# A position-wise convolution: weights of a group in one transfer of 128 rows, four weight buffers, windows asked for in mid row

## The chip, the core and the metric

The kernel runs on one core of one Trainium2 chip. The metric is the time of one execution on the device in microseconds (us). Three runs of the kernel before took 12917.63, 12935.22 and 12935.37 us; the median is 12935.22 us.

## What is computed

The reference works on `x` of shape (32, 32, 56, 56): batch, channels, height, width. It has two residual layers. The change concerns the first, a convolution with 3 x 3 patches whose weights are not shared: each of the 56 x 56 positions has its own matrix of 32 output channels by 288 patch elements.

```python
K, STRIDE, PAD, C_IN, C_OUT, OUT_H, OUT_W, BATCH = 3, 1, 1, 32, 32, 56, 56, 32
IN_DIM, POSITIONS = C_IN * K * K, OUT_H * OUT_W
weight: (C_OUT, POSITIONS, IN_DIM)
...
patches = _unfold(x, K, STRIDE, PAD).transpose(0, 2, 1)   # batch, position, 288
out = jnp.einsum('bpi,opi->bop', patches, weight)
out = out + bias[None, :, :]
...
x = x + _L0_conv_ref(_gn(x), L0_conv_weight, L0_conv_bias)
x = x + _L1_conv_ref(_gn(x), ...)
```

`_gn` normalises each channel of each image. The second layer searches for each position the 16 nearest other positions by their channels, weighs them with a softmax, and puts the result through a matrix and a batch normalisation.

## The kernel before

The program is a chain of stages, each with its own instructions on every engine and a barrier between two of them: `normalise_input`, `convolve`, `prepare`, `split_halves`, `attend`, `normalise_output`. Only `convolve` (from L135) is changed. Everything is float32 there.

`normalise_input` leaves the normalised image in device memory as `xg`, laid out channel, row, image, column, with a border of one row and one column of zeros.

`convolve` cuts the 56 rows of the image into four quarters of 14 rows (PER = 4, QH = 14, QN = 784 positions to a quarter) and works on the same row of all four quarters at once. So the 128 partitions of a weight tile are 4 quarters (q) of 32 output channels (o). It walks 14 rows, each of 56 positions. Four neighbouring positions (SLOTS = 4), for all four quarters, are a group here; a row has 14 groups (7 CHUNKS, two groups u = 0, 1 in each), the stage 196.

What each engine does in `convolve`:

- **SP** issues all loads. At the start of a row it asks for `windows` (L198): for each of the three kernel rows k one transfer, 32 channels by 4 quarters by one padded row of 32 images (7424 bytes). Windows have two buffers, one for even and one for odd rows; the wait in L196 is for the products of the row before the one at hand. Then, for each group, it waits until the buffer of two groups ago has been turned (L202) and issues four transfers (L205), one for each quarter: 32 output channels, each with 4 x 288 numbers that lie together (4608 bytes), into 32 partitions of `w_in[:, u]`.
- **PE** waits for the group's four transfers (L240), and turns the weights, position by position, with three transposes each (L233) from 128 partitions of (q, o) to 96 partitions of (k, channel). With the turned weights as the stationary side it then multiplies (L253): for each position 12 small products, 3 kernel columns by 4 quarters, 96 rows deep, 32 output channels by 32 images. Two positions are turned ahead (AHEAD = 2), so in each group PE has 9 transposes in a row, 24 products, 3 transposes, and 72 products (the order of its instructions is the same in both kernels but for line numbers). `turned` counts turned positions; SP and ACT wait on it.
- **ACT** copies the turned weights of a position out of PSUM into `w_turned` (L272).
- **DVE** copies the results of a group from PSUM into `conv_sb` (L284), one copy for each group.
- At the end SP stores `conv_sb` in four transfers, one for each quarter (L212).

The order of the work is that of the loops as written; the engines meet at semaphores alone. SP runs as far ahead of PE as the buffers allow: `turned` starts with a credit of 2 x SLOTS (TURN_FREE, L168).

Of the kernel before, what the change touches and what calls it, by code (L numbers as in the profile page):

```python
# [5 lines left out]
FP32 = mybir.dt.float32  # L6
# [6 lines left out]
BATCH, C, H, W = 32, 32, 56, 56  # L13
N = H * W
K = 3
IN_DIM = C * K * K
NEIGHBOURS = 16
P = 128
# [116 lines left out]
def convolve(nc, weight, xg, conv):  # L135


    SLOTS = 4
    AHEAD = 2
    CHUNKS = W // (2 * SLOTS)  # L140
    KC = K * C
    with ExitStack() as stack:
        enter = stack.enter_context
        windows = enter(nc.sbuf_tensor("windows", [KC, 2, PER, BATCH * WP], FP32))
        w_in = enter(nc.sbuf_tensor("w_in", [P, 2, SLOTS, IN_DIM], FP32))
        w_turned = enter(nc.sbuf_tensor("w_turned", [KC, 4, K * P], FP32))
        conv_sb = enter(nc.sbuf_tensor("conv_sb", [P, BATCH, QN], FP32))
        ident = enter(nc.sbuf_tensor("ident_c", [P, P], FP32))
# [2 lines left out]
        ident_ready = enter(nc.semaphore("c_ident"))  # L151
        win0 = enter(nc.semaphore("c_win0"))
        win1 = enter(nc.semaphore("c_win1"))
        w0 = enter(nc.semaphore("c_w0"))
        w1 = enter(nc.semaphore("c_w1"))
        turned = enter(nc.semaphore("c_turned"))
        wt_ready = enter(nc.semaphore("c_wt_ready"))
        multiplied = enter(nc.semaphore("c_multiplied"))
# [1 line left out]
        out_stored = enter(nc.semaphore("c_out"))  # L160
        passed = enter(nc.semaphore("c_passed"))
        block = enter(nc.Block())
        win_loaded, w_loaded = [win0, win1], [w0, w1]
        xg_rows = xg.rearrange("c h b w -> c h (b w)")
        weight_rows = weight.rearrange("o p i -> o (p i)")


        TURN_FREE, WT_FREE, MUL_FREE, COPY_FREE = 2 * SLOTS, SLOTS, 2 * W * PER, 2  # L168

        def each_half(engine, body):  # L170


            with engine.Fori(0, QH // 2) as t:
                for r in range(2):
                    row = t * 2 + r
                    body(row, None, None, r, None)
                    with engine.Fori(0, CHUNKS) as j:
                        for u in range(2):
                            body(row, (row * CHUNKS + j) * (2 * SLOTS) + u * SLOTS, j, r, u)

        def each_half_written_out(engine, body):

            with engine.Fori(0, QH // 2) as t:
                for r in range(2):
                    row = t * 2 + r
                    body(row, None, None, r, None)
                    for j in range(CHUNKS):
                        for u in range(2):
                            body(row, row * W + (j * (2 * SLOTS) + u * SLOTS), j, r, u)

        @block.sync
        def _(sp):
            def body(row, before, j, r, u):
                if u is None:

                    sp.wait_ge(multiplied, row * (W * PER) + W * PER)  # L196
                    for k in range(K):
                        sp.dma_start(windows[k:KC:K, r, :, :],  # L198
                                     xg_rows[:, bass.ds(row + k, PER, QH), :]).then_inc(win_loaded[r], 16)
                    return  # L200

                sp.wait_ge(turned, before + SLOTS)  # L202
                for q in range(PER):
                    at = (row * W + j * (2 * SLOTS) + (u * SLOTS + q * QN)) * IN_DIM
                    sp.dma_start(w_in[C * q:C * (q + 1), u, :, :].rearrange("o s i -> o (s i)"),  # L205
                                 weight_rows[:, bass.ds(at, SLOTS * IN_DIM)]).then_inc(w_loaded[u], 16)

            each_half(sp, body)
            for q in range(PER):

                sp.wait_ge(copied, QN // SLOTS + COPY_FREE)
                sp.dma_start(conv[:, :, q * QN:(q + 1) * QN].rearrange("b c n -> c b n"),  # L212
                             conv_sb[C * q:C * (q + 1), :, :]).then_inc(out_stored, 16)
            sp.wait_ge(out_stored, 16 * PER)
# [9 lines left out]
        def _(pe):  # L224
# [8 lines left out]
                    last = nc.tensor.transpose(w_ps[0:KC, s, k * P:(k + 1) * P], w_in[:, u, s, k::K], ident[:])  # L233
                last.then_inc(turned, 1)

            def body(row, before, j, r, u):
                if u is None:
                    gate(pe, win_loaded[r], (row - r) * (8 * K) + 16 * K, passed)
                    return
                pe.wait_ge(w_loaded[u], (row * CHUNKS + j) * (16 * PER) + 16 * PER)  # L240
                for s in range(AHEAD):
                    turn(before, s, u)

                pe.wait_ge(copied, (row * CHUNKS + j) * 2 + (u + 1))
                for s in range(SLOTS):
                    if s + AHEAD < SLOTS:
                        turn(before, s + AHEAD, u)

                    pe.wait_ge(wt_ready, before + (s + 1 + WT_FREE))
                    for k in range(K):  # L250
                        for q in range(PER):
                            x_k = windows[:, r, q, :].rearrange("p (b w) -> p b w", w=WP)[:, :, j * (2 * SLOTS) + (u * SLOTS + s + k)]
                            last = nc.tensor.matmul(conv_ps[C * q:C * (q + 1), u, s, 0:BATCH],  # L253
                                                    w_turned[:, s, k * P + C * q:k * P + C * (q + 1)], x_k,
                                                    start=k == 0, stop=k == K - 1)
                            if k == K - 1:
                                last.then_inc(multiplied, 1)
# [1058 lines left out]
```

## Time and profile before

| | us |
|---|---|
| median of three runs | 12935.22 |
| the profiled execution, its own time | 12949.0 |
| span of its trace | 12947.2 |
| PE busy in the span | 9126.0 |
| DVE busy | 11081.8 |
| ACT busy | 10096.9 |
| first weight transfer issued in `convolve` | 203.1 |
| first store of its result issued | 1157.8 |
| transposes of weights (L233), 2352 of them, PE busy | 375.1 |
| products (L253), 18816 of them, PE busy | 363.9 |

The profiled execution is 14 us above the median. Times within the trace are counted from the start of the span. Busy time is the time in which an engine executes; a transfer is issued by a queue (SPq) and carried by the core's 16 DMA engines, whose mean busy share the profile gives for any stretch, with packets by size. Each transfer also leaves small packets that report its completion. The granted clock of PE (PEclk) is given as a share of its full speed: 1.0 is 2.4 GHz, 0.5 is 1.2 GHz.

### The profile page before, as it was taken

The page shows a single profiled execution, that of the slowest core. Times are in us where ns is not written, and L with a number is a line of the kernel's source. Part 1 is how long each engine was busy: PE and PEld are TensorE (multiplying, and loading weights), DVE is VectorE, ACT ScalarE, POOL GpSimd, SP SyncE. Part 2 cuts the span into 40 slices and gives each one's busy share as a digit, 9 for nine tenths or more (in the row PEclk, how much of TensorE's full clock was granted, in tenths as well). Part 3 has the DMA queues.
Part 4 walks back from the last instruction along what each step waited for, and adds up shares of the span by engine and source line. Part 5 has one row for each costly group of instructions (what it writes and reads, how often), then busy time and mean ns, then how long its engine had stood idle before and what let it go on. Part 6 is the DMA issues. An engine that isn't in the chain of part 4 may idle for free. (4 is left out here: it accounts for less than half of the span.)

```text
span 12947.2 us, 304970 instructions
## 1 busy us (share of the span) xinstructions
PE 9126.0 (70%) x105146; PEld 5952.5 (46%) x105146; DVE 11081.8 (86%) x24921; ACT 10096.9 (78%) x11352; POOL 2951.5 (23%) x1648
## 2 busy tenths in 40 slices
PE   2775577777777777777777777777777777767765
PEld 2664344444444444444444444444444444444443
DVE  1001599999999999999999999999999999999997
ACT  2332488888888888888888888888888888878876
POOL 0000022222222222222222222222222222222221
PEclk9887788888887888888888888888888788878877
DMA  9666700000000000000000000000000000000003
GB/s 145 166 169 177 229 3 15 16 15 16 15 16 15 16 15 16 15 4 16 15 16 15 15 15 15 15 15 15 15 15 3 15 15 16 15 15 15 15 3 122
DMA packets 267458, 479.24 MB, mean 37 GB/s; under 512 B 196964, under 2 KB 197348, under 8 KB 248356
## 3 DMA queue, kind: packets, MB, share of 16 engines
q1 hardware_dynamic: 261348, 407.82, 13.4%
q0 software_dynamic: 4608, 51.38, 1.1%
q8 instruction: 944, 15.47, 0.5%
q14 instruction: 558, 4.57, 0.1%
HBM read 353.59 MB, written 105.50 MB: 35 GB/s over the span
## 5 line engine op out<-in xcount | busy, mean ns | idle before, releaser
L819 POOL TENSOR_TENSOR masked<-masked,shares_a 128x784 f32<-128x784 f32 x1600 | 2930.9, 1854 | 8335.2 <-DVE top L1091 8305.1
L870 PE MATMUL psum<-ident_a,masked 128*128 128x128 f32 (+1 forms) x20000 | 3600.4, 317 | 872.7 <-ACT turned_sb L983 788.0
L983 ACT ACTIVATE turned_sb<-psum 128x512 f32<-128x512 f32 (+1 forms) x5600 | 3040.3, 555 | 1461.6 <-PE psum L870 1443.9
L870 PEld LDWEIGHTS psum<-ident_a,masked 128*128 128x128 f32 (+1 forms) x20000 | 2518.3, 160 | 2497.7 <-issue 2410.6
L1052 DVE MAX8 found<-scores 128x8 f32<-128x224 f32 x11200 | 3435.0, 376 | 115.6 <-ACT scores L962 83.1
L1091 DVE CUSTOM_DVE_ANT_0 masked<-masked,scores 128x3136 f32<-128x3136 f32 x800 | 2740.2, 3425 | 27.5
L889 PE MATMUL psum<-turned_sb,rows 128*32 128x128 f32 (+1 forms) x40000 | 2024.2, 342 | 769.3 <-ACT inverse_sb L970 769.3
L962 ACT ACTIVATE scores<-psum 128x1568 f32<-128x1568 f32 x1600 | 2354.6, 1472 | 176.3 <-DVE top L1091 144.9
L974 ACT ACTIVATE masked<-masked,minus_top 128x3136 f32<-128x3136 f32 x800 | 2348.0, 2935 | 0.0
L954 ACT ACTIVATE masked<-shares_a,own 128x3136 f32<-128x3136 f32 x800 | 2322.7, 2903 | 1.0
L889 PEld LDWEIGHTS psum<-turned_sb,rows 128*32 128x32 f32 (+1 forms) x40000 | 1555.1, 137 | 1136.9 <-issue 1136.9
L847 PE MATMUL psum<-points 32*128 32x392 f32 x12800 | 1787.4, 633 | 76.2 <-issue 33.8
L1083 DVE SCALAR_TENSOR_TENSOR scores<-scores,bound,shares_a 128x1568 f32<-128x1568 f32 x800 | 1473.9, 1842 | 0.0
L858 PE MATMUL psum<-ones,above 128*1 128x1 f32 x1600 | 150.7, 163 | 1341.8 <-DVE rest L1132 1340.7
L284 DVE COPY conv_sb<-conv_ps 128x128 f32 x196 | 57.1, 291 | 953.8 <-PE conv_ps L253 953.8
L272 ACT ACTIVATE w_turned<-w_ps 96x384 f32<-96x384 f32 x784 | 343.7, 486 | 646.8 <-PE w_ps L233 644.3
L1082 DVE TENSOR_SCALAR scores<-scores,bound 128x1568 f32<-128x1568 f32 x800 | 813.1, 1016 | 3.6 <-DVE bound L1073 2.4
L858 PEld LDWEIGHTS psum<-ones,above 128*1 128x1 f32 x1600 | 90.0, 80 | 1512.6 <-issue 1512.6
L847 PEld LDWEIGHTS psum<-points 32*128 32x128 f32 x12800 | 566.9, 207 | 394.1 <-issue 394.0
L233 PE MATMUL w_ps<-ident_c,w_in 128*96 128x128 f32 x2352 | 375.1, 299 | 438.8 <-DMA w_in<-in_L_conv_weight_dram 437.3
L851 PE MATMUL psum<-halves_a,minus 3*128 3x392 bf16 x6400 | 644.6, 379 | 0.0
L1128 DVE SCALAR_TENSOR_TENSOR bound_low<-over,best,margin 128x2 f32<-128x2 f32 x800 | 583.5, 729 | 28.5
(135 smaller groups left out, 5714.9 us busy)
## 6 DMA issues: line engine op xcount, KB each, us to landing
w_in<-in_L_conv_weight_dram SPq DMA_DIRECT2D x784, 144.0 KB, 2.8
points<-unit SPq DMA_DIRECT2D x128, 392.0 KB
shares_a<-share SPq DMA_DIRECT2D x32, 1568.0 KB
windows<-xg SPq DMA_DIRECT2D x42, 928.0 KB, 11.6
xg<-padded SPq DMA_DIRECT2D x32, 406.0 KB, 18.7
table<-table_sb SPq DMA_DIRECT2D x32, 404.2 KB
rows<-table SPq DMA_DIRECT2D x32, 396.0 KB
x_in<-in_x_dram POOLq DMA_DIRECT2D x8, 1568.0 KB, 13.1
```

Source lines behind the costliest of these rows:

```text
L819: nc.gpsimd.tensor_tensor(m, m, shares[:, t.half, k * width:(k + 1) * width], ALU.add).then_inc(logits_ready, 1)
L847: nc.tensor.matmul(ps[:, r * BANK:r * BANK + SCH], points[C * r:C * (r + 1), t.half, t.queries()], points[C * r:C * (r + 1), t.half, at:at ...
L870: last = nc.tensor.transpose(ps[0:width, bank + u * P:bank + (u + 1) * P], masked[:, t.ring, j * P:j * P + width], ident[:])
L889: last = nc.tensor.matmul(ps[q:q + C, SUM_BANK:SUM_BANK + P], rows[0:width, t.half, j, 0:C], turned_sb[0:width, t.par, j, :], start=j < PE ...
L954: nc.scalar.activation(masked[:, t.ring, :], shares[:, t.half, :], ACT.Relu, bias=own[:, t.half, at:at + 1], scale=STEEP / SLOPE).then_inc ...
L962: nc.scalar.activation(scores[:, t.par, quad * QUAD:(quad + 1) * QUAD].rearrange("p (a b) -> p a b", b=SCH), ps[:, 0:PER * BANK].rearrange ...
L974: nc.scalar.activation(masked[:, t.ring, :], masked[:, t.ring, :], ACT.Exp, bias=minus_top[:, t.ring:t.ring + 1], accum_out=total[:, t.rin ...
L983: nc.scalar.activation(turned_sb[0:high, t.par, g * GROUP:g * GROUP + width // P, :].rearrange("p a b -> p (a b)"), ps[0:high, bank:bank + ...
L1052: n = step(nc.vector.max(found[:, t.par, c, :], scores[:, t.par, c * PART:(c + 1) * PART]))
L1082: step(nc.vector.tensor_scalar(low, low, bound[:, 0:1], 0.0, ALU.subtract, ALU.min))
L1083: return step(nc.vector.scalar_tensor_tensor(high, high, bound[:, 0:1], shares[:, t.half, POOL_COLS:N], ALU.subtract, ALU.min))
L1091: nc.vector.tensor_tensor_reduce(m, m, scores[:, t.par, :], 1.0, NEVER, ALU.add, ALU.max, top[:, 0:1]).then_inc(masked_ready, 1)
```

## The change

Three things change in `convolve`, and nothing else. The four transfers for a group's weights are now one, whose source is the weights seen as quarter, output channel, run of 4608 bytes, and whose destination is all 128 partitions of a buffer. `w_in` has four buffers (DEEP) instead of two, each with a semaphore of its own that counts 16 for a transfer, and `turned` starts with a credit of four groups. SP's program is written out instead of looped: it asks for the windows of the first row, and then, in each row but the last, for the windows of the next row ahead of the chunk j = 3 (its seventh group). `deep` gives the buffer of a group and the number of times that it has been filled.

```diff
--- before.py
+++ after.py
@@ -136,13 +136,14 @@
 
 
     SLOTS = 4
+    DEEP = 4
     AHEAD = 2
     CHUNKS = W // (2 * SLOTS)
     KC = K * C
     with ExitStack() as stack:
         enter = stack.enter_context
         windows = enter(nc.sbuf_tensor("windows", [KC, 2, PER, BATCH * WP], FP32))
-        w_in = enter(nc.sbuf_tensor("w_in", [P, 2, SLOTS, IN_DIM], FP32))
+        w_in = enter(nc.sbuf_tensor("w_in", [P, DEEP, SLOTS, IN_DIM], FP32))
         w_turned = enter(nc.sbuf_tensor("w_turned", [KC, 4, K * P], FP32))
         conv_sb = enter(nc.sbuf_tensor("conv_sb", [P, BATCH, QN], FP32))
         ident = enter(nc.sbuf_tensor("ident_c", [P, P], FP32))
@@ -151,8 +152,7 @@
         ident_ready = enter(nc.semaphore("c_ident"))
         win0 = enter(nc.semaphore("c_win0"))
         win1 = enter(nc.semaphore("c_win1"))
-        w0 = enter(nc.semaphore("c_w0"))
-        w1 = enter(nc.semaphore("c_w1"))
+        w_loaded = [enter(nc.semaphore(f"c_w{k}")) for k in range(DEEP)]
         turned = enter(nc.semaphore("c_turned"))
         wt_ready = enter(nc.semaphore("c_wt_ready"))
         multiplied = enter(nc.semaphore("c_multiplied"))
@@ -160,12 +160,14 @@
         out_stored = enter(nc.semaphore("c_out"))
         passed = enter(nc.semaphore("c_passed"))
         block = enter(nc.Block())
-        win_loaded, w_loaded = [win0, win1], [w0, w1]
+        win_loaded = [win0, win1]
         xg_rows = xg.rearrange("c h b w -> c h (b w)")
-        weight_rows = weight.rearrange("o p i -> o (p i)")
-
-
-        TURN_FREE, WT_FREE, MUL_FREE, COPY_FREE = 2 * SLOTS, SLOTS, 2 * W * PER, 2
+        weight_rows = weight.rearrange("o (q p) i -> q o (p i)", q=PER)
+
+
+        GROUPS_PER_LAP = 2 * W // SLOTS // DEEP
+
+        TURN_FREE, WT_FREE, MUL_FREE, COPY_FREE = DEEP * SLOTS, SLOTS, 2 * W * PER, 2
 
         def each_half(engine, body):
 
@@ -183,29 +185,37 @@
             with engine.Fori(0, QH // 2) as t:
                 for r in range(2):
                     row = t * 2 + r
-                    body(row, None, None, r, None)
+                    body(t, row, None, None, r, None)
                     for j in range(CHUNKS):
                         for u in range(2):
-                            body(row, row * W + (j * (2 * SLOTS) + u * SLOTS), j, r, u)
+                            body(t, row, row * W + (j * (2 * SLOTS) + u * SLOTS), j, r, u)
+
+        def deep(t, r, j, u):
+
+            n = (r * CHUNKS + j) * 2 + u
+            return n % DEEP, t * GROUPS_PER_LAP + (n // DEEP + 1)
 
         @block.sync
         def _(sp):
-            def body(row, before, j, r, u):
-                if u is None:
-
-                    sp.wait_ge(multiplied, row * (W * PER) + W * PER)
-                    for k in range(K):
-                        sp.dma_start(windows[k:KC:K, r, :, :],
-                                     xg_rows[:, bass.ds(row + k, PER, QH), :]).then_inc(win_loaded[r], 16)
-                    return
-
-                sp.wait_ge(turned, before + SLOTS)
-                for q in range(PER):
-                    at = (row * W + j * (2 * SLOTS) + (u * SLOTS + q * QN)) * IN_DIM
-                    sp.dma_start(w_in[C * q:C * (q + 1), u, :, :].rearrange("o s i -> o (s i)"),
-                                 weight_rows[:, bass.ds(at, SLOTS * IN_DIM)]).then_inc(w_loaded[u], 16)
-
-            each_half(sp, body)
+            def load_windows(row):
+
+                sp.wait_ge(multiplied, row * (W * PER) + W * PER)
+                for k in range(K):
+                    sp.dma_start(windows[k:KC:K, row % 2, :, :],
+                                 xg_rows[:, bass.ds(row + k, PER, QH), :]).then_inc(win_loaded[row % 2], 16)
+
+            load_windows(0)
+            for row in range(QH):
+                for j in range(CHUNKS):
+                    if j == CHUNKS // 2 and row + 1 < QH:
+                        load_windows(row + 1)
+                    for u in range(2):
+                        first = row * W + j * (2 * SLOTS) + u * SLOTS
+
+                        sp.wait_ge(turned, first + SLOTS)
+                        k, _ = deep(0, row % 2, j, u)
+                        sp.dma_start(w_in[:, k, :, :].rearrange("p s i -> p (s i)"),
+                                     weight_rows[:, :, first * IN_DIM:(first + SLOTS) * IN_DIM]).then_inc(w_loaded[k], 16)
             for q in range(PER):
 
                 sp.wait_ge(copied, QN // SLOTS + COPY_FREE)
@@ -233,18 +243,19 @@
                     last = nc.tensor.transpose(w_ps[0:KC, s, k * P:(k + 1) * P], w_in[:, u, s, k::K], ident[:])
                 last.then_inc(turned, 1)
 
-            def body(row, before, j, r, u):
+            def body(t, row, before, j, r, u):
                 if u is None:
                     gate(pe, win_loaded[r], (row - r) * (8 * K) + 16 * K, passed)
                     return
-                pe.wait_ge(w_loaded[u], (row * CHUNKS + j) * (16 * PER) + 16 * PER)
+                k_in, lap = deep(t, r, j, u)
+                pe.wait_ge(w_loaded[k_in], lap * 16)
                 for s in range(AHEAD):
-                    turn(before, s, u)
+                    turn(before, s, k_in)
 
                 pe.wait_ge(copied, (row * CHUNKS + j) * 2 + (u + 1))
                 for s in range(SLOTS):
                     if s + AHEAD < SLOTS:
-                        turn(before, s + AHEAD, u)
+                        turn(before, s + AHEAD, k_in)
 
                     pe.wait_ge(wt_ready, before + (s + 1 + WT_FREE))
                     for k in range(K):
```

On SP, at the border between two rows of the image in the kernel before (`w_in` holds weights of a group, `windows` the patches of a row; what an instruction waits for stands in brackets):

```order
L205 DMA w_in<-in_L_conv_weight_dram 32x1152
L177 REGISTER_ALU
L177 COMPARE_AND_BRANCH
L196 ISA
L198 DMA windows<-xg 32x4x1856 [waits c_multiplied]
L198 DMA windows<-xg 32x4x1856
L198 ISA
L198 DMA windows<-xg 32x4x1856
L177 UNCONDITIONAL_BRANCH
L177 ISA
L205 ISA [waits c_turned]
L205 DMA w_in<-in_L_conv_weight_dram 32x1152
```

The three transfers of the windows stand behind the last weights of the row and ahead of the first of the next; the weights come in transfers of 32 rows.

On SP now, from the first row's windows to the first row's seventh group and on:

```order
L204 DMA windows<-xg 32x4x1856 x2
L217 DMA w_in<-in_L_conv_weight_dram 128x1x1152 [waits c_turned] x6
L204 DMA windows<-xg 32x4x1856 [waits c_multiplied]
L204 DMA windows<-xg 32x4x1856 x2
L217 DMA w_in<-in_L_conv_weight_dram 128x1x1152 [waits c_turned] x14
```

The windows of the second row stand ahead of the first row's seventh group, those of the third row 14 groups further on, and so forth; a group has one transfer into 128 partitions.

## Rows read from the trace of the kernel before

**Rows 1.** SP's queue in order of time (start us, us, engine, line, xcount [idle]).

```profile
...
203.10 65.32 SPq L205 DMA_DIRECT2D w_in<-in_L_conv_weight_dram  x56
...
677.61 2.59 SPq L198 DMA_DIRECT2D windows<-xg  x3
...
1157.84 29.04 SPq L212 DMA_DIRECT2D conv<-conv_sb  x4
...
```

**Rows 2.** Waits of the stage 203 to 1157 us: total us, times, longest.

```profile
...
PE w_ps L233 <- DMA w_in<-in_L_conv_weight_dram: 437.3, 93, 218.5
...
```

**Rows 3.** DVE in order of time around the end of an image row.

```profile
...
701.67 0.29 DVE L284 COPY conv_sb<-conv_ps 128x128 f32 x1 [17.91 <-PE conv_ps L253]
...
709.01 0.29 DVE L284 COPY conv_sb<-conv_ps 128x128 f32 x1 [3.65 <-PE conv_ps L253]
712.46 0.29 DVE L284 COPY conv_sb<-conv_ps 128x128 f32 x1 [3.15 <-PE conv_ps L253]
716.39 0.29 DVE L284 COPY conv_sb<-conv_ps 128x128 f32 x1 [3.64 <-PE conv_ps L253]
...
```

**Rows 4.** Busy times by stretch: us and count by engine, PEclk, DMA share, GB/s.

```profile
...
684.00:698.00 14.00, 1.38 (x7) 1.31 (x8) 0.00 (x0) 0.38 (x1) 0.00 (x0) 0.59 0.93 205
698.00:702.00 4.00, 4.00 (x110) 3.09 (x109) 0.29 (x1) 1.60 (x5) 0.00 (x0) 0.74 0.17 48
702.00:720.00 18.00, 17.10 (x541) 14.15 (x540) 1.36 (x5) 8.63 (x20) 0.00 (x0) 1.00 0.59 166
...
```

**Rows 5.** DMA, 684 to 696 us, where the windows travel.

```profile
...
DMA packets 571, 2.69 MB, mean 224 GB/s; under 512 B 129, under 2 KB 129, under 8 KB 570
...
q1 hardware_dynamic: 570, 2.67, 101.0%
...
```

**Rows 6.** DMA, 703 to 743 us, with only weights on the way.

```profile
...
DMA packets 2013, 6.31 MB, mean 158 GB/s; under 512 B 668, under 2 KB 668, under 8 KB 2004
...
q1 hardware_dynamic: 2004, 6.16, 54.7%
...
```

**Rows 7.** DMA, 1520.5 to 1525 us, two stores of 4 rows.

```profile
...
DMA packets 20, 0.10 MB, mean 23 GB/s; under 512 B 11, under 2 KB 11, under 8 KB 12
...
half_sq<-half_sb SPq DMA_DIRECT2D x1, 49.0 KB
...
```

**Rows 8.** DMA, 12850 to 12857 us, loads into 128 partitions.

```profile
...
DMA packets 257, 2.95 MB, mean 421 GB/s; under 512 B 22, under 2 KB 22, under 8 KB 22
...
q1 hardware_dynamic: 257, 2.95, 99.9%
...
```

**Rows 9.** DMA, 1160 to 1195 us, stores out of 32 partitions each.

```profile
...
DMA packets 2325, 7.19 MB, mean 205 GB/s; under 512 B 32, under 2 KB 32, under 8 KB 2325
...
q1 hardware_dynamic: 2325, 7.19, 97.0%
...
```

**Rows 10.** DMA of the whole stage, 203 to 1157 us.

```profile
...
q1 hardware_dynamic: 43646, 155.32, 62.7%
...
w_in<-in_L_conv_weight_dram SPq DMA_DIRECT2D x784, 144.0 KB, 2.8
windows<-xg SPq DMA_DIRECT2D x39, 928.0 KB, 11.7
```

**Rows 11.** PE in order of time, 675 to 752 us.

```profile
...
696.62 2.16 PE L233 MATMUL w_ps<-ident_c,w_in 128*96 128x128 f32 x9 [13.46 <-DMA w_in<-in_L_conv_weight_dram]
...
712.55 1.23 PE L233 MATMUL w_ps<-ident_c,w_in 128*96 128x128 f32 x9 [0.41 <-DMA w_in<-in_L_conv_weight_dram]
...
714.26 0.57 PE L233 MATMUL w_ps<-ident_c,w_in 128*96 128x128 f32 x3
...
```

**Rows 12.** By tile, `w_in`, then `windows`: ns min/median/max, first and last start.

```profile
...
L233 PE MATMUL w_ps<-ident_c,w_in x2352: 272/273/461, 218.5 to 1155.7; 128*96 128x128 f32 x196
...
L205 SPq DMA_DIRECT2D w_in<-in_L_conv_weight_dram x784: 315/316/1802, 203.1 to 1149.7; - x196
...
L198 SPq DMA_DIRECT2D windows<-xg x42: 579/605/1412, 200.2 to 1084.8; - x42
...
```

## The prediction

> **What bounds the kernel now.** I read the page first, for the share of the stage: the convolution runs from the first weight transfer at 203.1 us to its first store at 1157.8 us [rows 1], 955 us of 12947, and nothing outside it is touched. Inside it I asked three things in this order: who waits, what a row of the image looks like in time, and how fast the DMA engines run.
>
> The waits of the stage [rows 2] show PE held by `w_in` for 437.3 us; 218.5 us of that is one piece, the time up to the first transpose of the program, and 219 us in 92 pieces lie within the stage. So the weights are late, not the matmuls. The copies on DVE [rows 3] give the pitch: where nothing is late two copies stand 3.45 us apart; the next comes 3.93 us later (a short wait for weights, at about every second group); and once in a row of 14 groups there is a hole of 17.91 us. SP's queue [rows 1] says what the hole is: the three `windows` transfers are issued at 677.61 us, behind all weights of the row, and the weights of the next row only behind them. From 684 to 698 us PE does nothing but its last 1.4 us, its granted clock falls to 0.5 (the 1.2 GHz level), and it is back at 1.00 only after 702 us [rows 4], while the DMA engines are full: 224 GB/s at a share of 101% [rows 5]. One row of the image thus takes 955/14 = 68.2 us: 14 x 3.45 = 48.3 us of pure PE pitch, and about 20 us of holes.
>
> **What the change moves.** (1) Four transfers of 32 rows become one of 128 rows. (2) `w_in` gets four buffers, so a group's weights may be asked for four groups ahead, not two. (3) The windows of the next row are asked for ahead of a row's seventh group instead of behind its last.
>
> If nothing else happened, (2) and (3) would take most of the 20 us out. But (1) decides, because it fixes on how many DMA engines the weights travel, and here I expect the opposite of a gain.
>
> *What the trace shows on that.* A stretch with only weights holds 2004 data and completion packets of that queue, 668 of them small: two data packets of 4608 bytes for each completion [rows 6]. A transfer of 32 rows therefore makes 16 shares of two rows, each with its completion. In the stage `prepare` there are stores of only 4 rows (`half_sq`, `share`). Two of them leave 20 packets in their window, 8 of 12.5 KB and at most 11 small ones, where 16 shares each would leave 32 [rows 7]. So a transfer whose outermost count is 4 does not get 16 shares. The new source is `o (q p) i -> q o (p i)`: its outermost count is q = 4, then 32, then one run of 4608 bytes; only the SBUF side counts 128. The old ones, and `windows`, count 32 outermost on both sides. I take it that the split goes by the outermost count that both sides have in common, 4, so that a group's 128 rows go to four DMA engines, 32 rows each, one q per engine. The Trainium skill says this outright (DMA: Bandwidth & Descriptors, on how many engines a DMA uses): the number of engines is the largest up to 16 that divides the slowest dimension of both access patterns. The rows agree for 4 rows and for 32; no row here has a 4 on one side only. By the same page's other advice, one 128-partition transfer in place of several, one would expect the first rival below.
>
> *The price of a group on four engines.* Each of the four carries 32 x 4608 B = 147.5 KB per group. How fast one engine is depends on whom it shares with, and the trace of before has no transfer on four engines, so I bound it by rows:
> - Best: loads of 128 rows in the last stage, 421 GB/s on 16 full engines, 26.3 GB/s each [rows 8]: 5.6 us.
> - Worst: stores out of 32 partitions, 205 GB/s at a share of 97.0%, 13.2 GB/s each [rows 9]: 11.2 us.
> - Nearest: the same rows in the same 4608 B pieces, 1336 x 4608 B = 6.16 MB in 54.7% of 16 x 40 us: 17.6 GB/s for a busy engine [rows 6]: 8.4 us.
>
> The second is half of the first: engines that serve the same few partitions can halve each other. With four engines on four blocks of 32 partitions there are fewer neighbours than with 16 engines on one block, so I go below 8.4; but a transfer has landed only with the slowest of its four, so I stay above the middle of 5.6 and 8.4. I take 7.5 us (estimated). The Trainium skill gives a reason for the halving (SBUF — State Buffer, on the DMA port swizzle): partitions 0 to 31 and 32 to 63 reach the same eight ports. By that rule two engines that walk two such blocks in step would get half each, which is the third rival below.
>
> `windows` still counts 32 outermost and goes over all 16: 3 x 928 KB = 2.85 MB in a row [rows 10], 178 KB per engine. At 26.3 GB/s this takes 6.8 us, at the 14 GB/s per engine of [rows 5] it takes 12.7 us; I take the middle, 9.8 us, since twelve engines have nothing else to do and run ahead.
>
> *The sum.* 7.5 us is over twice PE's pitch of 3.45 us, so four engines bound the stage, and they never rest: with three more groups in their queue (22 us) the time from a turned buffer to its next transfer is hidden, and so is the landing of 2.8 us [rows 10]. PE's group stays under 7.5 us even at the low clock (the first one behind the hole took 701.67 + 0.29 - 696.62 = 5.3 us [rows 3, 11]). Row of the image: 14 x 7.5 + 9.8 = 114.8 us, 14 rows: 1607 us. From 203.1 us, with 2.8 us to land and 5.3 us for the last group, the stage ends at about 1818 us instead of 1158 us: +660 us. The profiled execution took 12949.0 us (span 12947.2), so 13609 us; the median of the runs is 14 us below it, so **13595 us**.
>
> *Edits that I cost at nothing.* SP issues one transfer of about 0.6 us (the median of `windows`, which has 128 pieces too) instead of four of 0.32 us [rows 12]. The deeper buffers and the earlier windows stay correct but cannot help a queue that is full anyway: the windows cost their bytes wherever they stand. Their wait in mid row is for the products of the row before, done before the third group of this row is turned, so the weights behind it on SP are not held. PE has one wait per group as before; what it issues is the same. The stages behind start later and run as they did.
>
> **The rivals.**
> 1. *All 16 engines carry it* (the split goes by the 128 rows, or by all 4 x 32). Against it: [rows 7]. For it: bytes and rows are the same as before. Then the weights of a group cost 590 KB/16 at 17.6 GB/s = 2.1 us, a row 14 x 2.1 + 12.7 = 42 us of DMA under 48.3 us of PE, and PE bounds. The windows in mid row still push in front of the weights: 12.7 + 2.1 + 2.8 = 17.6 us, against a cover of four buffers, 4 x 3.45 - 2.3 (until a group is turned, 714.26 + 0.57 - 712.55 [rows 11]) = 11.5 us; a hole of 6.1 us stays. 14 x 48.3 + 13 x 6.1 = 756 us against the 939 us from the first transpose at 218.5 us [rows 12] to 1157.8: -183 us, **12752 us**. This is the way to the other side, and it decides from the point where a group takes less than 68.2/14 = 4.9 us of DMA, windows included.
> 2. *Four engines that never meet.* 5.6 us a group, windows 6.8 us: 14 x (14 x 5.6 + 6.8) = 1193 us, stage end 1404, +246 us, **13181 us**. For it: they write four different blocks of partitions. Against: the two nearest rows are slower.
> 3. *Four engines in step, in pairs.* 11.2 us a group, windows 12.7 us: 2373 us, end 2584, +1426 us, **14361 us**. For it: [rows 9]. Against: the windows between the rows of the image load the four engines unequally and pull the pairs apart. The port rule of the Trainium skill named above would make it so for as long as the pairs keep step.
>
> **Chances.** Four engines with partial sharing (my forecast) 0.60, four undisturbed 0.20, four in step 0.14, all 16 engines 0.06. A measurement of this kernel tells about 0.2% (26 us) from no change; no case lies within that, I leave it 0.01. Slower 0.94, faster 0.05. The range runs from the undisturbed case, 13170 us, to 14050 us, where a group takes about 9.6 us with 12.7 us for the windows; outside are the 16 engines and most of the case in step.
>
> **What would show it.** In the stage: three quarters of the small completion packets gone and more (4 for a transfer of 128 rows); the time from issue to landing of `w_in` up from 2.8 us to some 25 to 30 us; the queue's share of the stage down from 62.7% [rows 10] to about 30%, at some 95 GB/s; copies on DVE evenly 7 to 8 us apart with a longer hole where the windows pass; PE waiting for `w_in` about 1000 us, its clock mostly at 0.5. If instead `w_in` lands within 10 us and the copies stand 3.45 us apart, it went over 16 engines and I am wrong. If the copies stand 5.6 or 11 us apart, only the sharing is mis-sized.

## The result and the profile after

| | us |
|---|---|
| after, median of 6 runs | 13279.72 (13274.52 to 13301.59) |
| before, median of 6 runs | 12932.22 (12917.63 to 12935.37) |
| ratio | 1.0272, interval 1.0259 to 1.0285 |

The change makes the kernel 2.7% slower, by 347 us. The profiled execution has a span of 13281.1 us, 334 us above that of before.

From the page of the profile of the changed kernel: the span, the products' copies, the transposes and the weight transfers (busy us, mean ns, then idle time and its releaser):

```profile
span 13281.1 us, 302260 instructions
...
q1 hardware_dynamic: 249588, 407.77, 12.0%
...
L295 DVE COPY conv_sb<-conv_ps 128x128 f32 x196 | 57.2, 292 | 1295.8 <-PE conv_ps L264 1295.8
...
L243 PE MATMUL w_ps<-ident_c,w_in 128*96 128x128 f32 x2352 | 484.8, 361 | 679.9 <-DMA w_in<-in_L_conv_weight_dram 657.3
...
w_in<-in_L_conv_weight_dram SPq DMA_DIRECT2D x196, 576.0 KB
...
```

There are 196 weight transfers of 576 KB instead of 784 of 144 KB; their time to landing is not on the page any more. SP's queue, in order of time (start us, us), answers to [rows 1]:

```profile
...
187.18 2.04 SPq L204 DMA_DIRECT2D windows<-xg  x3
...
310.26 9.56 SPq L204 DMA_DIRECT2D windows<-xg  x3
319.87 82.25 SPq L217 DMA_DIRECT2D w_in<-in_L_conv_weight_dram  x14
...
1332.71 6.37 SPq L204 DMA_DIRECT2D windows<-xg  x3
...
1493.31 29.02 SPq L222 DMA_DIRECT2D conv<-conv_sb  x4
...
```

The stage reaches from 187.2 us (the first windows) to 1493.3 us (the first store): 1306.1 us. Before, it reached from 200.2 us [rows 12] to 1157.8 us [rows 1]: 957.6 us. It is 348.5 us longer. It began 13 us earlier; the stage in front of it is the same in both kernels, and its end moves by as much between sets of runs (in the twelve experiments below the first windows are issued at 185 to 189 us in eight, at 203 to 204 us in the four of the last set), so this is not the change's doing. What follows the stage takes 11788 us after (13281.1 - 1493.3) and took 11789 us before (12947.2 - 1157.8). From 310.26 to 1332.71 us lie 11 rows of the image: 92.9 us each, where they were 68.2.

DMA between two passages of the windows, 806 to 864 us (the same view as [rows 6]):

```profile
...
DMA packets 1375, 6.25 MB, mean 108 GB/s; under 512 B 40, under 2 KB 40, under 8 KB 1367
...
q1 hardware_dynamic: 1367, 6.11, 25.6%
...
```

Of 1367 packets 40 are small: 33 data packets to one completion packet, where there were two. And the queue's share of 16 engines is 25.6%, that of four full ones, whatever PE does. DVE's copies there, in order of time, answer to [rows 3]:

```profile
...
817.02 0.29 DVE L295 COPY conv_sb<-conv_ps 128x128 f32 x1 [12.60 <-PE conv_ps L264]
821.46 0.29 DVE L295 COPY conv_sb<-conv_ps 128x128 f32 x1 [4.15 <-PE conv_ps L264]
827.07 0.29 DVE L295 COPY conv_sb<-conv_ps 128x128 f32 x1 [5.32 <-PE conv_ps L264]
833.84 0.29 DVE L295 COPY conv_sb<-conv_ps 128x128 f32 x1 [6.49 <-PE conv_ps L264]
838.25 0.29 DVE L295 COPY conv_sb<-conv_ps 128x128 f32 x1 [4.11 <-PE conv_ps L264]
...
867.43 0.29 DVE L295 COPY conv_sb<-conv_ps 128x128 f32 x1 [5.22 <-PE conv_ps L264]
...
```

From 817.02 to 867.43 us lie nine distances (four copies are left out): 5.60 us on average, each between 4.4 and 6.9. In the kernel before it was 3.45 and 3.93 in turn. Busy times by stretch (PE, PEld, DVE, ACT, POOL; PEclk, DMA share, GB/s), over the stage, while windows travel, and between:

```profile
...
190.00:1490.00 1300.00, 809.13 (x21069) 645.23 (x21069) 56.88 (x195) 362.12 (x782) 0.00 (x0) 0.76 0.37 122
778.00:790.00 12.00, 5.08 (x132) 3.89 (x123) 0.58 (x2) 1.95 (x4) 0.00 (x0) 0.63 1.00 226
792.00:864.00 72.00, 48.43 (x1196) 38.69 (x1197) 3.21 (x11) 21.07 (x45) 0.00 (x0) 0.69 0.26 106
...
```

For 12 to 13 us in a row of the image all 16 engines are full; for the rest four are, at 106 GB/s. The windows are not through by then. DMA from 777.5 to 790.5 us, then from 791 to 802 us:

```profile
...
DMA packets 491, 2.91 MB, mean 224 GB/s; under 512 B 37, under 2 KB 37, under 8 KB 490
...
q1 hardware_dynamic: 490, 2.89, 98.7%
...
```

```profile
...
DMA packets 192, 1.06 MB, mean 96 GB/s; under 512 B 16, under 2 KB 16, under 8 KB 191
...
q1 hardware_dynamic: 191, 1.04, 25.7%
...
```

The packets tell the two kinds apart, 7424 bytes for windows and 4608 for weights. In the first stretch the windows of twelve engines (288 packets, 2.14 MB) leave 165 packets and 0.75 MB, 4.5 KB each: weights. In the second, on four engines, 175 packets hold 1.04 MB, 5.9 KB each, so about 83 of them are windows, most of the 96 that four engines have to carry. So twelve engines carry their windows first and the four carry theirs behind weights. PE's waits within the stage (total us, times, longest us):

```profile
...
PE w_ps L243 <- DMA w_in<-in_L_conv_weight_dram: 438.0, 176, 9.9
...
PE w_ps L243 <- issue: 22.4, 6, 4.2
...
```

### The profile page after: what moved, and what is told of

Same layout as the page of the kernel before. It is cut to its first block and busy times, and to the rows that moved or that the text cites. A ratio compares the mean times of both kernels' runs of the same rounds, so it can differ in the third digit from the quotient of the medians.

```text
span 13281.1 us, 302260 instructions
## 1 busy us (share of the span) xinstructions
PE 9191.7 (69%) x105146; PEld 6022.6 (45%) x105146; DVE 11076.4 (83%) x24921; ACT 10129.5 (76%) x11352; POOL 2948.8 (22%) x1648
## 3 DMA queue, kind: packets, MB, share of 16 engines
q0 software_dynamic: 4608, 51.38, 1.1%
## 5 line engine op out<-in xcount | busy, mean ns | idle before, releaser
L881 PE MATMUL psum<-ident_a,masked 128*128 128x128 f32 (+1 forms) x20000 | 3480.9, 310 | 961.7 <-ACT turned_sb L994 877.4
L881 PEld LDWEIGHTS psum<-ident_a,masked 128*128 128x128 f32 (+1 forms) x20000 | 2439.6, 156 | 2546.7 <-issue 2458.1
L900 PE MATMUL psum<-turned_sb,rows 128*32 128x128 f32 (+1 forms) x40000 | 2162.9, 359 | 801.3 <-ACT inverse_sb L981 801.3
L900 PEld LDWEIGHTS psum<-turned_sb,rows 128*32 128x32 f32 (+1 forms) x40000 | 1659.3, 144 | 1183.1 <-issue 1183.0
L858 PE MATMUL psum<-points 32*128 32x392 f32 x12800 | 1750.8, 614 | 53.2 <-ACT scores L973 21.8
L243 PE MATMUL w_ps<-ident_c,w_in 128*96 128x128 f32 x2352 | 484.8, 361 | 679.9 <-DMA w_in<-in_L_conv_weight_dram 657.3
L243 PEld LDWEIGHTS w_ps<-ident_c,w_in 128*96 128x96 f32 x2352 | 346.4, 180 | 735.7 <-DMA w_in<-in_L_conv_weight_dram 464.8
```

The source lines that it names most:

```text
L858: nc.tensor.matmul(ps[:, r * BANK:r * BANK + SCH], points[C * r:C * (r + 1), t.half, t.queries()], points[C * r:C * (r + 1), t.half, at:at ...
L881: last = nc.tensor.transpose(ps[0:width, bank + u * P:bank + (u + 1) * P], masked[:, t.ring, j * P:j * P + width], ident[:])
L900: last = nc.tensor.matmul(ps[q:q + C, SUM_BANK:SUM_BANK + P], rows[0:width, t.half, j, 0:C], turned_sb[0:width, t.par, j, :], start=j < PE ...
```

## The experiments

Three theories stood at the start. **A**: the transfer runs on four DMA engines, because its source counts four outermost. **B**: the deeper buffers or the windows in mid row cost the time. **C**: a transfer of 128 rows out of two nested strides is slow as such. All times are medians; the runs of one table row were measured beside the kernel before on the same chip, and the ratio is to that.

| run | time, us | ratio (interval) | stage, us |
|---|---|---|---|
| four transfers of 32 rows, else as changed | 12895.8 | 0.9970 (0.9959 to 0.9981) | 907.6 |
| the one transfer alone | 13465.7 | 1.0409 (1.0391 to 1.0426) | 1484.3 |
| channel outermost | 12894.0 | 0.9969 (0.9956 to 0.9981) | 910.6 |
| windows at the border | 13283.2 | 1.0267 (1.0250 to 1.0284) | 1302.8 |
| two transfers of 64 rows | 14377.8 | one run | 2393.0 |
| as changed, windows cut | 13247.3 | one run | 1132.6 |
| channel outermost, windows cut | 12915.7 | one run | 797.4 |
| channel outermost, windows apart | 12887.0 | 0.9960 (0.9948 to 0.9973) | 905.6 |
| mid row alone | 12963.5 | 1.0009 (1.0000 to 1.0019) | 965.8 |
| four buffers alone | 12899.6 | 0.9958 (0.9942 to 0.9975) | 908.7 |
| order restored by ACT, windows apart | 12888.2 | 0.9949 (0.9932 to 0.9965) | 890.9 |
| the same, PE written out | 12822.2 | 0.9902 (0.9886 to 0.9919) | 848.0 |

The stage is that of one profiled execution, from the first windows issued to the first store issued.

### Only the transfer undone

```diff
-                        sp.dma_start(w_in[:, k, :, :].rearrange("p s i -> p (s i)"),
-                                     weight_rows[:, :, first * IN_DIM:(first + SLOTS) * IN_DIM]).then_inc(w_loaded[k], 16)
+                        for q in range(PER):
+                            sp.dma_start(w_in[C * q:C * (q + 1), k, :, :].rearrange("p s i -> p (s i)"),
+                                         weight_rows[q, :, first * IN_DIM:(first + SLOTS) * IN_DIM]).then_inc(w_loaded[k], 16)
...
-                pe.wait_ge(w_loaded[k_in], lap * 16)
+                pe.wait_ge(w_loaded[k_in], lap * (16 * PER))
```

> Undoes the transfer alone: four transfers of 32 rows again, with four buffers and the windows in mid row kept. If the weights lost their time to running on four DMA engines (theory A), they are back on 16: row of the image 14 x 3.45 us of PE plus a hole of about 6 us where the windows pass, 12750 us, 3 data packets or fewer per completion packet. If the deeper buffers or the windows in mid row cost the time (theory B: they push 2.85 MB in front of weights that are needed first), it stays near 13280 us.

12895.8 us: the whole loss of 347 us is gone, and 38 us more. B falls. But the gain is a fifth of the 183 us that the first rival of the prediction gave for 16 engines; that is taken up below.

### Only the transfer made

The kernel before, with `weight_rows` as changed and one transfer for each group into `w_in[:, u]`, which counts 16 instead of 64.

> The kernel before with the one transfer of 128 rows alone: two buffers, windows at the row's border. Theory A: four engines, 5.6 us a group and not always fed by two buffers (up to 6.5 us), the windows and their stall uncovered, 97 to 110 us a row, 13330 to 13520 us, forecast 13400. Theory B: the transfer is harmless, 12930 us or a little less.

13465.7 us, within A's range and 66 us above its forecast. Between the windows, 640 to 690 us, by stretch (columns as above):

```profile
...
640.00:690.00 50.00, 33.78 (x837) 26.38 (x839) 2.03 (x7) 14.78 (x31) 0.00 (x0) 0.71 0.25 93
...
```

Two buffers feed the four engines only in part: 93 GB/s instead of 106, with dips to between 29 and 55 GB/s among slices of 103 and more (DMA view of the same 50 us). Beside the run below with the windows at the border too, which takes 13283.2 us, the four buffers save 182 us of what the transfer costs; in the changed kernel they are what keeps the engines full.

### The channel outermost

```diff
-        weight_rows = weight.rearrange("o (q p) i -> q o (p i)", q=PER)
+        weight_rows = weight.rearrange("o (q p) i -> o q (p i)", q=PER)
...
-                                                    w_turned[:, s, k * P + C * q:k * P + C * (q + 1)], x_k,
+                                                    w_turned[:, s, k * P + q:(k + 1) * P:PER], x_k,
```

> As changed, one transfer of 128 rows, but with the output channel outermost (32) and the quarter inside (4); partition 4o + q instead of 32q + o, and the products read every fourth column of the turned weights. Theory A: 32 outermost on the source, so 16 engines: at most 2.1 us of DMA a group, PE bounds, 12700 to 12760 us. Theory C (a transfer of 128 rows from two nested strides is slow as such, whatever their order): about 13280 us. If the strided columns slow the weight loads on PE, up to 100 us on top.

12894.0 us. It is still one transfer of the same 128 rows from two nested strides; only the order of the strides is another, and 386 us go. C falls. Its DMA view from 640 to 655 us (GB/s in 40 equal slices):

```profile
...
GB/s 61 184 418 406 307 56 0 0 0 0 0 98 98 123 344 406 393 111 44 0 0 0 221 61 295 393 430 204 12 0 0 98 98 160 356 418 369 74 44 0
DMA packets 565, 2.36 MB, mean 157 GB/s; under 512 B 64, under 2 KB 64, under 8 KB 561
...
```

The weights come in bursts of up to 430 GB/s, four times the steady 106 of the changed kernel, and 561 packets of that queue hold 64 small ones, a completion packet to every eight data packets: 16 shares of eight rows.

### The windows back at the border

> As changed, but the windows asked for at the start of their row again. Theory A: four engines are full either way, a row costs the same bytes, 13280 us within 40, rather above it (the first weights of a row wait for the windows). Theory B: this takes the cost out, towards 12930 us.

`load_windows(row)` stands at the start of its row again, nothing else is changed. 13283.2 us against 13279.7: no difference. Where they stand costs and gives nothing as long as four engines bound the stage, as the prediction had it.

### Two transfers of 64 rows

```diff
+                        for q in range(0, PER, 2):
+                            sp.dma_start(w_in[C * q:C * (q + 2), k, :, :].rearrange("p s i -> p (s i)"),
+                                         weight_rows[q:q + 2, :, first * IN_DIM:(first + SLOTS) * IN_DIM]).then_inc(w_loaded[k], 16)
```

> As changed, but a group's weights in two transfers of 64 rows, source counts 2 x 32. If the outermost count sets the number of engines (theory A), each runs on two engines, and both on the same two: 64 rows of 178 ns each per engine, 11.4 us a group, about 160 + 15 us a row of the image, stage some 2400 us, time about 14400 us. If the split were by rows or bytes (theory C), smaller transfers would be no slower: 13280 us or less.

14377.8 us, 22 us from the forecast of A, and the stage 2393 us against 2400. DMA from 1000 to 1050 us, and SP's first and last issue:

```profile
...
DMA packets 594, 2.70 MB, mean 54 GB/s; under 512 B 18, under 2 KB 18, under 8 KB 590
...
q1 hardware_dynamic: 590, 2.64, 12.8%
...
```

```profile
...
188.86 2.06 SPq L204 DMA_DIRECT2D windows<-xg  x3
...
2581.84 29.02 SPq L223 DMA_DIRECT2D conv<-conv_sb  x4
...
```

12.8% of 16 engines is two of them, and 572 data packets stand against 18 small ones, 32 to one. Cutting the transfer in two halves the speed instead of leaving it: both halves go to the same two engines. With 4 (25.6%), 2 (12.8%) and 32 (bursts on all) outermost, A is shown. The rule of the Trainium skill that the prediction quoted (DMA: Bandwidth & Descriptors, on how many engines a DMA uses) holds here for a 4 and a 2 on the source side alone, which no row of before could show.

### The windows cut, on four engines

```diff
-                    sp.dma_start(windows[k:KC:K, row % 2, :, :],
-                                 xg_rows[:, bass.ds(row + k, PER, QH), :]).then_inc(win_loaded[row % 2], 16)
+                    if row < 2:
+                        sp.dma_start(windows[k:KC:K, row % 2, :, :],
+                                     xg_rows[:, bass.ds(row + k, PER, QH), :]).then_inc(win_loaded[row % 2], 16)
+                    else:
+                        sp.dma_start(windows[k:KC:K, row % 2, 0, 0:128],
+                                     xg_rows[:, row + k, 0:128]).then_inc(win_loaded[row % 2], 16)
```

> As changed, but from the third row on the three window transfers bring only 512 bytes a channel instead of four quarters of 7424 (the products there run on stale patches): the price of the weights alone on four engines. 14 x 5.6 = 78 us a row instead of 92.5, some 175 us less than 13280: 13105 us. If the groups cost more than the packets show, it stays above 13150.

The time, 13247.3 us, is 142 us above the forecast, but the stage is where it was expected. SP's queue:

```profile
...
184.83 2.03 SPq L205 DMA_DIRECT2D windows<-xg  x3
...
307.19 6.20 SPq L208 DMA_DIRECT2D windows<-xg  x3
...
1171.62 5.31 SPq L208 DMA_DIRECT2D windows<-xg  x3
...
1317.46 29.04 SPq L226 DMA_DIRECT2D conv<-conv_sb  x4
...
```

The stage takes 1132.6 us, 173.5 less than as changed (175 forecast), and 11 rows 864.4 us, 78.6 each: 5.61 us a group. So a passage of windows costs 92.9 - 78.6 = 14.3 us. The rest of the kernel is longer by 140 us, probably (no run tests it) since stale patches put other data into the search for neighbours, where DVE has a branch that depends on them (`settle_doubts`); for the two runs with cut windows only the stage is read.

### The windows cut, on 16 engines

The same edit in the version with the channel outermost. It was to find what became of the 183 us.

> The version with the output channel outermost (16 engines), with the windows of the third row on cut down to 512 bytes a channel in the same way (stale patches). Theory D (there PE is held by its own instruction fetch while the windows fill all 16 DMA engines): without them the pieces of idle time with no releaser go, a row takes 49 to 51 us instead of 64.5, 12705 us. Theory E (PE is held by something else, say the strided weight loads or ACT): above 12850 us.

SP's first and last issue of the stage:

```profile
...
184.99 2.03 SPq L205 DMA_DIRECT2D windows<-xg  x3
...
982.34 28.07 SPq L226 DMA_DIRECT2D conv<-conv_sb  x4
...
```

The stage takes 797.4 us instead of 910.6 (again only the stage counts). That is 113 us less, 9.4 for each of the 12 passages, where 14 to 15 had been expected: a row takes 55.8 us, not 49 to 51, and with the windows 64.9. Where PE stands, in the version with four transfers of 32 rows and the windows in full (waits: total us, times, longest us):

```profile
...
PE conv_ps L265 <- issue: 96.1, 63, 5.3
...
PE w_ps L244 <- issue: 59.7, 16, 5.9
...
```

There is no row for `w_in` any more: PE waits 156 us for nothing that a semaphore shows. PE in order of time, 605 to 624 us, and the instruction queue in the DMA view, 606 to 618 us:

```profile
...
606.57 0.47 PE L265 MATMUL conv_ps<-windows,w_turned 96*32 96x32 f32 x17
612.31 0.33 PE L265 MATMUL conv_ps<-windows,w_turned 96*32 96x32 f32 x7 [5.27 <-issue]
...
617.25 0.29 PE L265 MATMUL conv_ps<-windows,w_turned 96*32 96x32 f32 x6
621.26 1.27 PE L265 MATMUL conv_ps<-windows,w_turned 96*32 96x32 f32 x66 [3.72 <-issue]
...
```

```profile
...
q1 hardware_dynamic: 573, 2.60, 100.5%
q8 instruction: 1, 0.02, 0.7%
...
```

PE stops after 17 of 24 products that wait for nothing, and again after 6 of 72, while the 16 engines are full with windows. In these 12 us one packet of instructions (q8) arrived; in 40 us without windows there were nine (2013 - 2004 packets [rows 6]), one every 4.4 us. Taken in steps of 1 us, the DMA view has q8 packets at 600, 609, 618 and 623 us: 9 us apart while the engines are full. PE resumes at 612.31 and 621.26 us, 2 to 3 us behind the second and the third. And between its two stops it runs 124 products and transposes, about what a packet holds: in the stage of the kernel before, 180 packets of q8 (2.95 MB, 16 KB each) arrive for 21168 of them, 118 to a packet. The profile does not name the engine of a q8 packet; that they are PE's rests on these counts. With the windows cut the same two waits are

```profile
...
PE w_ps L247 <- issue: 31.7, 11, 5.0
PE conv_ps L268 <- issue: 24.6, 32, 3.7
```

56 us in place of 156 (137 in the version with the channel outermost). So the hole that the four buffers had closed for the weights is opened again by PE's own instructions, which come over the same DMA engines. D holds for the larger part: the waits without a releaser fall by 81 us and the stage by 113. The 56 us that stay without windows are taken up with the last run.

### The windows apart from each other

```diff
-                    if j == CHUNKS // 2 and row + 1 < QH:
-                        load_windows(row + 1)
+                    if j in (2, 4, 6) and row + 1 < QH:
+                        load_windows(row + 1, [j // 2 - 1])
```

> The version with the output channel outermost, the three window transfers of the next row apart from each other, ahead of the 5th, 9th and 13th group instead of all ahead of the 7th. Theory D: each fills the DMA engines for 4 us only, shorter than PE's instructions last that are already fetched, so much of the hole goes: 12750 to 12850 us, below both kernels. Theory E: 12894 us, nothing.

12887.0 us, 7 us less than without (the two ratios' intervals overlap), where 45 to 145 had been expected. PE's waits without a releaser are 129 us instead of 137: three short passages hold the instructions up about as long as one long one; the forecast that a short one fits under the instructions already fetched was wrong.

### Mid row alone, four buffers alone

Both have the four transfers of 32 rows; one has `DEEP = 2`, the other four buffers and the windows at the border.

> The windows in mid row alone: four transfers of 32 rows, two buffers. Theory F (two buffers cover too little): 12.7 us of windows, 2.1 us of weights and 2.8 us of landing stand against a cover of 2 x 3.45 - 2.3 = 4.6 us, so the hole only moves from the border into the row: 12934 us within 20. Theory G (the hole came from standing at the border, where the windows themselves are waited for too): 30 us or more faster.

12963.5 us beside 12951.7 of before: within 20, as F had it. The hole moves into the row, and is no smaller: in the stage PE waits 172 us for `w_in` and 59 us without a releaser, before it was 219 and 12 us.

> The four buffers alone: four transfers of 32 rows, windows at the row's border. The short waits for weights inside a row (about 0.5 us at every second group, 3 us a row) go, 40 us; the hole stays, since the windows are waited for in full: they are asked for two groups earlier, 7 us less of it a row if PE's instructions come in time (12800 us), nothing if they are what is late there (12890 us).

12899.6 us beside 12951.7: 52 us less, near the case in which instructions are what is late. It is as fast as all but the transfer together (ratio 0.9958 against 0.9970, intervals overlapping): of the three parts of the change only the four buffers bring something.

### A version faster than both

```diff
-                    nc.scalar.activation(w_turned[:, s, :], w_ps[0:KC, s, 0:K * P], ACT.Copy).then_inc(wt_ready, 1)
+                    nc.scalar.activation(w_turned[:, s, :].rearrange("p (k q o) -> p k q o", k=K, q=PER),
+                                         w_ps[0:KC, s, 0:K * P].rearrange("p (k o q) -> p k q o", k=K, q=PER), ACT.Copy).then_inc(wt_ready, 1)
```

> As the version with the output channel outermost and the windows apart, but ACT writes the turned weights back in the order of the quarters, so that the products read 32 columns in a row again. The strided weight loads (161 ns against 127) cost about 0.1 us a group, 20 us in all: 12867 us. If ACT's copy gets slower by its strided read of PSUM and PE waits for it, 12890 us or more.

Beside 12951.7 us it took 12888.2. The stage is 890.9 us, 15 less than with strided weight loads (20 forecast), and a weight load takes 128 ns again instead of 161 (medians). The stages are of one profile each, and the times alone do not show the gain (ratio 0.9949 against 0.9960, intervals overlapping).

```diff
-            with engine.Fori(0, QH // 2) as t:
+            for t in range(QH // 2):
```

> As the run before, with PE's loop over pairs of rows written out in full. Theory H (six jumps back each cost a fetch of the loop's first instructions, about 5 us idle and 2 us at the low clock): 40 us less, 12825 us. Theory I (PE's instructions are late at the pace at which they are fetched, jump or not): the same as the run before.

12822.2 us, 66 less than the run before and 1.0% below the kernel before. The stage is 43 us shorter (40 forecast); the other 23 us lie outside it and are not explained. PE's waits without a releaser, first with the loop, then written out:

```profile
...
PE conv_ps L264 <- issue: 103.3, 49, 5.0
PE w_ps L243 <- issue: 38.9, 19, 5.2
...
```

```profile
...
PE conv_ps L264 <- issue: 95.2, 49, 4.4
...
PE w_ps L243 <- issue: 12.3, 8, 3.1
...
```

Those in front of the transposes, where a jump lands, fall from 38.9 to 12.3 us; those in mid stream stay, since the windows stay. With the loop, 30 of the 38.9 us are six waits of 4.9 to 5.2 us, after 28, 56, 84, 112, 140 and 168 of the 196 groups, where the loop jumps back; written out, PE waits 0.6 us at most at these places. The first of them:

```profile
...
350.80 2.16 PE L243 MATMUL w_ps<-ident_c,w_in 128*96 128x128 f32 x9 [5.16 <-issue]
...
```

The nine transposes behind it take 2.16 us instead of 1.20, at a granted clock of 0.50 (350 to 353 us). Six times 5.1 + 1.0 us is some 36 of the 43 us: H holds.

## Why the prediction was right, and where it was off

- **The split by the outermost count: right.** It was argued from two stores of four rows and the source's order; 25.6% of 16 engines, 33 packets to a completion, and the runs with 2 and 32 outermost show it.
- **7.5 us for a group on four engines: too high.** The sum's first term measured 5.61 us, the best end of its bounds. The step of the sum that failed is the reasoning between the rows: the halving of [rows 9] and the 8.4 us of [rows 6] were taken as near to the new case. The four engines write four blocks of 32 partitions at the full 26.3 GB/s each, as in [rows 8]; why they do not slow each other was not looked into. The case that was given 0.60, partial sharing, did not come about; the second rival, given 0.20, had this term right.
- **9.8 us for the windows: too low,** 14.3 us measured, more than the upper bound of 12.7. The reason given for the middle, that twelve engines run ahead, came true and did not help. While the twelve are full (13 us) the four engines move only 165 packets of weights, 14.6 GB/s each, instead of the 297 that they move in 13 us alone (1327 packets in 58 us): 5.8 us lost. Then they carry their own windows; 83 packets of them cost 7 us of the 11 us from 791 to 802 us, so all 96 cost about 8 us. Together these estimates, from one passage, give 13.9 us. The sum took 6.8 and 12.7 us as two bounds for one passage, where it had to add what the four lose during it to what they carry behind it.
- **The sum:** the first term is 14 x 1.9 = 26.5 us a row too high, the second 4.5 too low, so 22 us a row or 308 us in all; 660 - 308 = 352 against 348.5 measured in the stage. The forecast of +660 us is nearly twice the +347 us measured: the direction and the four engines were right, how they share and so the size were not. The two errors go against each other, and by this luck the forecast is 63 us (14 x 4.5) less wrong than its first term alone would make it. The result lies between the forecast (315 us below it) and the rival of four undisturbed engines (99 us above it), nearer to the rival.
- **The first rival** (16 engines, 12752 us) did not come, and its own price was wrong too: when the transfers do use 16 engines the time is 12894 to 12896 us. It counted waits for weights alone; PE then stood 137 to 156 us without a releaser, mostly for its instructions.
- **Four buffers and windows in mid row at nothing:** the windows' place is worth nothing, as said. The four buffers are worth 182 us, in that they keep the four engines fed, which the sum took for granted.
- **Signs in the profile.** The completion packets went as described; the DMA share of the stage, all queues together, fell from 0.64 to 0.37, not 0.3, at 122 GB/s. PE waited 438 us for `w_in`, not 1000, and its granted clock was 0.76 on average over the stage, not mostly 0.5, both at least in part because a group took 5.6 us and not 7.5. Copies stood 4.4 to 6.9 us apart away from the windows. The time to landing could not be read.

## What to carry to other kernels

Before several transfers become one, look at the outermost count of both sides: a source that counts 4 outermost and a destination of 128 partitions ran on four of 16 DMA engines, and the DMA share of a steady stretch (25%) tells it at a glance. Putting the larger count outermost, even if the partitions then stand in another order, brought the 16 back. When a stage's loads have stopped being late, look for idle time with no releaser in the midst of a run of instructions: a long written-out loop is fetched over the same DMA engines.

## What the runs showed of the hardware

- Two transfers whose source counts 2 outermost ran on two engines in all, not on two each: 12.8% of 16, 54 GB/s together with the instructions.
- Four engines moved 106 GB/s together, 26.3 GB/s each, while each wrote a block of 32 partitions of its own. 16 engines that store out of one such block at a time reached half of that each, 13.2 GB/s ([rows 9]).
- While twelve other engines carried windows, each of the four moved 14.6 GB/s of weights instead of 26.3 (777.5 to 790.5 us).
- Instructions arrive in pieces of 16 KB, one every 4.4 us in a stretch of this stage without windows. While bulk transfers filled all DMA engines, only one came in 12 us, and PE stood for up to 5.3 us in mid run.
- A jump back in PE's loop of 28 groups cost 4.9 to 5.2 us of idle time and 1 us at the lower clock, six times in the stage.
